# A hybrid block on one core: six more experts' weights in the tiles of x, whose rows pass through the first expert sum

## The reference

```python
probs = softmax(x @ router_w.T)                  # 64 experts
topk_w, topk_ids = top_k(probs, 8)               # 8 a token, at most 128 tokens an expert
xb = x_buf[:E * C].reshape(E, C, -1)             # gathered rows, 128 an expert
h = silu(einsum("ecd,edf->ecf", xb, w_gate)) * einsum("ecd,edf->ecf", xb, w_up)   # f = 192
y = einsum("ecf,efd->ecd", h, w_down)
routed = segment_sum(y[safe] * weight, tok)      # each row back to its token
shared = silu(sg) * su @ ws_down                 # a dense part for all tokens
x = x + routed + shared
```

## Time and profile before

| what | value |
|---|---|
| median of 3 runs | 2984.09 us (2981.26 to 2991.69) |
| profiled execution | 2984.79 us, span 2983.0 us |
| busy PE, DVE, ACT, POOL | 82%, 78%, 58%, 34% of the span |
| mean granted TensorE clock | 0.916 |
| DMA | 293.69 MB, mean 98 GB/s |
| shared part of f1 / expert loop of f1 | about 1602 to 1690 / 1690 to 1938 us |

### The profile page before, as it was taken

The page is one execution under the profiler, slowest core; times in us unless marked ns, Lnnn a source line. Parts: engine busy times, 40 slices in busy tenths (PEclk is TensorE's granted clock), DMA queues, the critical chain, the costliest instruction groups (busy, mean ns, idle before and its releaser), DMA issues. The chain is left out here.

```text
span 2983.0 us, 45953 instructions
## 1 busy us (share of the span) xinstructions
PE 2443.0 (82%) x14814; PEld 1084.2 (36%) x14814; DVE 2322.8 (78%) x3787; ACT 1715.9 (58%) x3510; POOL 1000.6 (34%) x755
## 2 busy tenths in 40 slices
PE   8899999999999999999767877737476676597772
PEld 5322222222222222222155566612122222456662
DVE  7898999999999999999158633338799998693333
ACT  3257888888888888888624322226465564532221
POOL 4500000000000000000202566652798996146662
PEclk9789999999999999999977998957899899598996
DMA  4423111111111111111434198770443441226997
GB/s 154 127 84 106 48 48 48 45 35 40 47 48 48 46 36 38 47 48 27 154 104 145 50 240 224 169 112 13 101 114 101 113 113 54 98 61 175 238 236 203
DMA packets 255164, 293.69 MB, mean 98 GB/s; under 512 B 39120, under 2 KB 210448, under 8 KB 254928
## 3 DMA queue, kind: packets, MB, share of 16 engines
q1 hardware_dynamic: 213664, 235.09, 27.4%
q0 software_dynamic: 33104, 46.42, 8.6%
q10 hardware_dynamic: 8160, 9.32, 1.0%
HBM read 223.35 MB, written 66.75 MB: 97 GB/s over the span
## 5 line engine op out<-in xcount | busy, mean ns | idle before, releaser
L745 DVE TENSOR_REDUCE att_mx<-att_pR 128x1 f32<-128x512 f32 x2048 | 1266.5, 684 | 33.5 <-PE att_pR L785 33.1
L728 ACT ACTIVATE att_probs<-att_pS 128x512 f32<-128x512 f32 x2048 | 1064.0, 603 | 231.2 <-PE att_pS L815 231.0
L832 PE MATMUL att_pA<-att_probs,att_vh 128*17 128x512 f32 x4096 | 539.5, 598 | 12.6 <-ACT att_acc_sb L709 12.2
L815 PE MATMUL att_pS<-att_q,att_k 64*128 64x512 bf16 x1344 | 458.0, 379 | 1.0 <-ACT att_probs L728 0.7
L2173 PE MATMUL sc_pY<-sc_hc,all_ident 128*128 128x512 f32 x512 | 263.4, 639 | 125.9 <-DVE sc_hc L2130 98.9
L2039 POOL TENSOR_TENSOR sc_bh<-ssm_du,sc_b 128x1024 f32<-128x1024 f32 x128 | 297.8, 2361 | 10.2 <-issue 5.6
L672 POOL TENSOR_TENSOR att_neg<-att_mx,att_minus 128x16 f32<-128x16 f32 x32 | 7.1, 223 | 842.4 <-DVE att_mx L753 842.4
L785 PE MATMUL att_pR<-head_k,head_q 64*128 64x512 bf16 x704 | 257.5, 403 | 13.7 <-PEq L71 7.1
L815 PE MATMUL att_pS<-head_q,head_k 64*128 64x512 bf16 (+1 forms) x1408 | 263.3, 381 | 0.2
L815 PE MATMUL att_pS<-att_qs,att_ks 64*128 64x512 bf16 x1344 | 261.1, 377 | 0.3
L785 PE MATMUL att_pR<-att_ks,att_qs 64*128 64x512 bf16 x672 | 259.3, 386 | 0.0
(11 more groups left out here) (303 smaller groups left out, 3884.5 us busy)
## 6 DMA issues: line engine op xcount, KB each, us to landing
sc_b<-scan_rows SPq DMA_DIRECT2D x128, 256.0 KB, 3.3
expert_sum<-att_zeros SPq DMA_DIRECT2D x4, 4224.0 KB, 21.2
f1e_wgu<-in_w_gate SPq DMA_DIRECT2D x64, 192.0 KB
f1e_wgu<-in_w_up SPq DMA_DIRECT2D x64, 192.0 KB
f2e_wgu<-in_w_gate SPq DMA_DIRECT2D x64, 192.0 KB
f2e_wgu<-in_w_up SPq DMA_DIRECT2D x64, 192.0 KB
sc_c<-scan_rows SPq DMA_DIRECT2D x40, 256.0 KB, 3.4
head_q<-query_parts SPq DMA_DIRECT2D x132, 64.0 KB, 2.2
```

Source lines behind the costliest of these rows:

```text
L728: act.activation(probs[:, k % (2 * HALF), :], bank(place(k)), ACT.Exp, scale=float(DK) ** -0.5).then_inc(expd, 1)
L745: dve.tensor_reduce(mx4[s][:, k // QC, k % QC:k % QC + 1], pR[:, (s + k) % 3, :], AX.X, ALU.max).then_inc(maxed, 1)
L815: mm = pe.matmul(bank(place(k)), kk[rows, t * P:(t + 1) * P], q[rows, c * GROUP:(c + 1) * GROUP], start=not half, stop=bool(half))
L832: mm = pe.matmul(pA[32 * c:32 * c + DK + 1, :], vh[s][:, t, :], probs[:, (HALF * g + j) % (2 * HALF), :], start=(t == 0), stop=(t == KT - ...
```

## The change

In `phase_experts`, once a pair of tiles of `x_sb` has got its shared part, ACT stores it to the first sum in HBM (`to_memory`; in place of the zeros there). Its tiles then hold the weights of six more experts, five tiles each (`more_at`: expert 10 + k goes to half k % 2, tile 5 (k // 2)), so that the ring has 16 slots. Before each of these six loads SP waits until the stores that cover its tiles, and all before them in that half, have landed. POOL waits for all stores before its first indirect addition, and clears the padding of the six slots. The test `if n == WR` in front of `both` is not touched. Since x now sits in the first sum, the state-space phase reads it with plain SP loads (two ahead of its weights, six behind) and POOL adds only the second sum; the final merge loads the first sum straight into `x_sb` and adds once per group.

```diff
-    WR = 10
+    OWN, MORE = 10, 6
+    WR = OWN + MORE
...
+        SLOT_TILES = 5
+        def more_at(k):
+            return k % 2, (k // 2) * SLOT_TILES
+        def more_flat(k):
+            h, t = more_at(k)
+            return x_sb[:, HT * h + t:HT * h + t + SLOT_TILES, :].rearrange("p t d -> p (t d)")
...
                     sp.wait_ge(listed, 1)
                     sp.dma_start(both[:, CAP:2 * CAP], firsts[EXPERTS:P, :]).then_inc(moved, 16)
+                if OWN <= n < WR:
+                    h, t = more_at(n - OWN)
+                    for k in range((t + SLOT_TILES + 1) // 2):
+                        sp.wait_ge(in_memory[h][k], 16)
                 if n >= WR:
                     sp.wait_ge(down, n - WR + 1)
...
             for n in range(LEAD):
                 gather(n)
+            for h in range(2):
+                for n in range(N):
+                    pool.wait_ge(in_memory[h][n], 16)
+            for k in range(MORE):
+                pool.memset(wd[OWN + k][H:P, 1, :], 0.0).then_inc(more_padded, 1)
...
+            def to_memory(n, h):
+                act.wait_ge(s_added, n * 2 + h + 1)
+                rows = slice(HT * h + n * 2, HT * h + n * 2 + 2)
+                act.dma_start(dst[:, rows, :], x_sb[:, rows, :]).then_inc(in_memory[h][n], 16)
+
             def shared_y(n, h):
+                if n >= 1:
+                    to_memory(n - 1, h)
                 act.wait_ge(s_down, v(n * 2 + (h + 1)))
-                if not early(n, 1):
-                    act.wait_ge(s_added, v(n * 2 + (h - 1)))
...
-            turns(act, shared, N, 2, 2, N - 2)
+            for n in range(N):
+                shared(n, n % 2, n // 2, N - 1 - n)
             for h in range(2):
                 shared_y(N - 1, h)
+            for h in range(2):
+                to_memory(N - 1, h)
...
                 for q in range(2):
                     dve.wait_ge(s_in[q][n], 16)
-                    if q:
-                        dve.wait_ge(added, 2 * n + 1)
-                    dve.tensor_tensor(row, row, part[:, n, q, :, :], ALU.add).then_inc(added, 1)
+                dve.tensor_tensor(row, row, part[:, n, :, :], ALU.add).then_inc(added, 1)
...
+            load(0)
+            load(1)
             sp.dma_start(wdt[:, :, :], io["W_dt"].rearrange("(c p) r -> p c r", p=P)).then_inc(w_in, 16)
...
+            for n in range(2, GROUPS):
+                load(n)
...
-            def merge(n, q):
-                if q:
-                    pool.wait_ge(merged[0][n], 16)
-                src = sums[q][0:TOK, :].rearrange("(t p) d -> p t d", p=P)
+            def merge(n):
+                pool.wait_ge(merged[0][n], 16)
+                src = sums[1][0:TOK, :].rearrange("(t p) d -> p t d", p=P)
...
             def first_merges():
-                for n in range(GROUPS):
-                    merge(n, 0)
                 for n in range(4):
-                    merge(n, 1)
+                    merge(n)
```

More of the change, by code:

```diff
@@ L1300, in phase_experts @@
         s_y = m.sb("s_y", [P, 2, 2 * D])
-        wgu = m.sb("wgu", [P, WR, DC, 2 * FF])
-        wd = m.sb("wd", [P, WR, 2, D])
+        own_wgu = m.sb("wgu", [P, OWN, DC, 2 * FF])
+        own_wd = m.sb("wd", [P, OWN, 2, D])
         xg = [m.sb(f"xg{s}", [P, ROW]) for s in range(R)]
@@ L1326, in phase_experts @@
         w_in = [m.sem(f"w_in{s}") for s in range(WR)]
+        in_memory = [[m.sem(f"in_memory{h}_{n}") for n in range(N)] for h in range(2)]
+        more_padded = m.sem("more_padded")
         consts = m.sem("consts")
@@ L1338, in phase_experts @@
         block = ctx.enter_context(nc.Block())
+        SLOT_TILES = 5
[4 more added lines that the diff above has]
+            return x_sb[:, HT * h + t:HT * h + t + SLOT_TILES, :].rearrange("p t d -> p (t d)")
+        wgu, wd = [], []
+        for k in range(OWN):
+            wgu.append(own_wgu[:, k, :, :])
+            wd.append(own_wd[:, k, :, :])
+        for k in range(MORE):
+            wgu.append(more_flat(k)[:, 0:DC * 2 * FF].rearrange("p (c n) -> p c n", c=DC))
+            wd.append(more_flat(k)[:, DC * 2 * FF:DC * 2 * FF + 2 * D].rearrange("p (c d) -> p c d", c=2))
         @block.sync
@@ L1355, in _ @@
                 for k, name in enumerate(("w_gate", "w_up")):
-                    sp.dma_start(wgu[:, w, :, k * FF:(k + 1) * FF], io[name][n].rearrange("(p c) f -> p c f", c=DC))                      .then_inc(w_in[w], 16)
-                sp.dma_start(wd[:, w, 0, :], io["w_down"][n, 0:P, :]).then_inc(w_in[w], 16)
-                sp.dma_start(wd[0:H, w, 1, :], io["w_down"][n, P:FF, :]).then_inc(w_in[w], 16)
+                    sp.dma_start(wgu[w][:, :, k * FF:(k + 1) * FF], io[name][n].rearrange("(p c) f -> p c f", c=DC))                      .then_inc(w_in[w], 16)
+                sp.dma_start(wd[w][:, 0, :], io["w_down"][n, 0:P, :]).then_inc(w_in[w], 16)
+                sp.dma_start(wd[w][0:H, 1, :], io["w_down"][n, P:FF, :]).then_inc(w_in[w], 16)
         @block.gpsimd
         def _(pool):
-            pool.memset(wd[H:P, :, 1, :], 0.0).then_inc(padded, 1)
+            pool.memset(own_wd[H:P, :, 1, :], 0.0).then_inc(padded, 1)
             pool.memset(hh[H:P, :, 1, :], 0.0).then_inc(padded, 1)
@@ L1416, in _ @@
         def _(act):
+            dst = sums[0][0:TOK, :].rearrange("(t p) d -> p t d", p=P)
+            def to_memory(n, h):
+                act.wait_ge(s_added, n * 2 + h + 1)
+                rows = slice(HT * h + n * 2, HT * h + n * 2 + 2)
+                act.dma_start(dst[:, rows, :], x_sb[:, rows, :]).then_inc(in_memory[h][n], 16)
             def shared_y(n, h):
+                if n >= 1:
+                    to_memory(n - 1, h)
                 act.wait_ge(s_down, v(n * 2 + (h + 1)))
-                if not early(n, 1):
-                    act.wait_ge(s_added, v(n * 2 + (h - 1)))
                 act.activation(s_y[:, h, :], pY[:, h, :], ACT.Copy).then_inc(s_y_ready, 1)
@@ L1555, in down_product @@
                 for c in range(2):
-                    mm = pe.matmul(pY[:, n % 2, 0:D], hh[:, n % 2, c, :], wd[:, n % WR, c, :],
+                    mm = pe.matmul(pY[:, n % 2, 0:D], hh[:, n % 2, c, :], wd[n % WR][:, c, :],
                                    start=(c == 0), stop=(c == 1))
@@ L1567, in _ @@
                 pe.wait_ge(w_in[w], 64 * (n // WR + 1))
+                if OWN <= n < WR:
+                    pe.wait_ge(more_padded, n - OWN + 1)
                 if n >= 2:
@@ L1571, in _ @@
                     for c in range(DC):
-                        mm = pe.matmul(pG[:, q, k * CAP:(k + 1) * CAP], wgu[:, w, c, k * P:(k + 1) * P], xT[:, q, c * P:(c + 1) * P],
+                        mm = pe.matmul(pG[:, q, k * CAP:(k + 1) * CAP], wgu[w][:, c, k * P:(k + 1) * P], xT[:, q, c * P:(c + 1) * P],
                                        start=(c == 0), stop=(c == DC - 1))
@@ L1585, in phase_merge @@
         m = Mem(nc, ctx, tag)
-        part = m.sb("part", [P, GROUPS, 2, GT, D])
+        part = m.sb("part", [P, GROUPS, GT, D])
         s_in = [[m.sem(f"s_in{q}_{n}") for n in range(GROUPS)] for q in range(2)]
@@ L1596, in load @@
             src = sums[q][0:TOK, :].rearrange("(t p) d -> p t d", p=P)
-            eng.dma_start(part[:, n, q, :, :], group_of(src, n)).then_inc(s_in[q][n], 16)
+            eng.dma_start(part[:, n, :, :] if q else group_of(x_sb, n), group_of(src, n)).then_inc(s_in[q][n], 16)
         @block.sync
@@ L1604, in _ @@
             for n in range(GROUPS):
-                sp.wait_ge(added, 2 * n + 2)
+                sp.wait_ge(added, n + 1)
                 sp.dma_start(group_of(dst, n), group_of(x_sb, n)).then_inc(stored, 16)
@@ L1619, in _ @@
                     dve.wait_ge(s_in[q][n], 16)
-                    if q:
-                        dve.wait_ge(added, 2 * n + 1)
-                    dve.tensor_tensor(row, row, part[:, n, q, :, :], ALU.add).then_inc(added, 1)
-            dve.wait_ge(added, 2 * GROUPS)
+                dve.tensor_tensor(row, row, part[:, n, :, :], ALU.add).then_inc(added, 1)
+            dve.wait_ge(added, GROUPS)
 def ffn(nc, io, tag, x_sb, ident, table, sums, out):
@@ L1712, in _, with load @@
         def _(sp):
+            def load(n):
+                src = sums[0][0:TOK, :].rearrange("(t p) d -> p t d", p=P)
+                sp.dma_start(x_sb[:, n * GT:(n + 1) * GT, :], src[:, n * GT:(n + 1) * GT, :])\
+                  .then_inc(merged[0][n], 16)
+            load(0)
+            load(1)
             sp.dma_start(wdt[:, :, :], io["W_dt"].rearrange("(c p) r -> p c r", p=P)).then_inc(w_in, 16)
@@ L1733, in _ @@
         def _(pool):
-            def merge(n, q):
-                if q:
-                    pool.wait_ge(merged[0][n], 16)
-                src = sums[q][0:TOK, :].rearrange("(t p) d -> p t d", p=P)
+            def merge(n):
+                pool.wait_ge(merged[0][n], 16)
+                src = sums[1][0:TOK, :].rearrange("(t p) d -> p t d", p=P)
```

(8 more changed lines are left out.)

## The result

The changed kernel takes 3023.03 us (median of four runs, 3015.68 to 3023.65) beside 2985.64 for the kernel before (four runs): a ratio of 1.0118, 95% interval 1.0094 to 1.0142. The forecast was 3029.4, a rise of 44.6 us where 37.4 was measured. The profiled execution has a span of 3021.0, 38.0 over that of before.

What follows compares the result with a forecast made beforehand. Expert loops were taken as DMA-bound beside a shared part with idle DMA. 25.3 + 24.6 + 1.4 - 7.5 + 0.5 + 1.5 - 1.2 = +44.6 on 2984.8 gives 3029.4 us; eight times in ten 3013 to 3041.

Steps and rivals of the forecast that it cites:

- The held list chain: Hand-over to experts: `both` follows expert 15's weights, behind the last stores; first gather later by 25.3 (f1) and 24.6 us (f2).
- the time at which `both` leaves: Hand-over: SP issues `both` 6.4 us after the last shared addition, about 1696.1 in f1, with a store taken at 2.5.
- the queue ahead of `both`: Hand-over: `both` queues behind the weights of experts 14 and 15; 0.7 us a stage, +1.4, bounds 0 and 2.5 a stage.
- The worst case of 5 us a stage: Hand-over: all 1.15 MB of weights still ahead of `both` in its ring, the sum some 9 us higher.
- The loop: Expert loops: 48 experts' weights left to load, not 54; six experts move to 3.19 us each, together -7.5.
- POOL's 3.19: Tail of the expert loop: once the last weights are in, POOL's own two issues pace it at 3.19 us.
- The rival in which bytes count in full: Expert loops: bound by the bytes of the whole loop, 15.2 us saved a stage, total 3006; chance 8%.
- Covered work: Both stages: stores, unrolled ACT loop and POOL memsets are hidden and cost nothing; uncovered stores would be 8 us a stage.
- the longer pause of PE: Before the experts: PE idles some 30 us and not 5; costs nothing more, 2 us a stage at the most.
- the 0.5 us of more semaphores to clear: Both stages: twenty-three more semaphores to clear in each, +0.5 us in all, bounds 0 and 3.
- The entry of the state space: After f1: POOL's fourth merge waits for SP's fourth load, and DVE for POOL's root; +1.5 us, bounds -1 and +6.
- The final merge: After f2: one addition of 1.23 us behind the last load and not two; -1.2, bounds -2 and 0.

Runs made afterwards that it cites:

- Experiment 1: Changed kernel with one condition altered, so that `both` is issued after expert 9's weights (n == OWN) as in the kernel before: 2979.46 us, ratio 0.9987.
- 2: Kernel before with only an added SP wait for the last shared addition ahead of `both`: 3015.56 us, ratio 1.0110.
- experiment 3: Changed kernel with four extra slots (MORE = 4), so that `both` follows expert 13: 2993.59 us, ratio 1.0042.
- 4: Changed kernel with `both` issued after the waits of expert 14 but ahead of the weights of experts 14 and 15: 3012.53 us, ratio 1.0105.
- experiment 6: Experiment 1 without the transfer of w_gate for experts 16 to 63, computing with wrong gate weights: 2956.15 us, one run.
- Experiment 5: Changed kernel with no extra slot (MORE = 0), rows still passing through the first sum and `both` following expert 9: 2983.6 us, ratio 0.9996.
- experiment 9: Experiment 1 with SP's loads of groups 0 to 3 ahead of the small weights and POOL's memset of `sel` ahead of its first merge: 2969.7 us, ratio 0.9949.

## Why the forecast held, point by point

**The held list chain: right, shown.** The forecast rested on reading that an untouched `if n == WR` moves with WR. It named the order on SP's queue, the stores as what is waited for, and 26.0 and 25.3 us. It was 24.3 and 24.4. Experiment 1 takes it away, 2 makes it alone, 3 scales it, 4 splits it. The two uncertain terms, the time at which `both` leaves and the queue ahead of it, were both sized a little high. A store of 256 KB landed in 2.1 us and not 2.5:

```profile
expert_sum<-all_x ACTq DMA_DIRECT2D x32, 256.0 KB, 2.1
```

and `both` left 5.6 us after the last addition (1689.36 + 1.26 = 1690.62), not 6.4. The queue ahead of `both`, set at 0.7 a stage, was 0.2 to 0.3: it landed in 2.0 and 2.1 us, beside 1.8 in the kernel before. The worst case of 5 us a stage did not come, though experiment 3, with 2.7 and 3.6 us, shows that the term need not be small. The order within a ring that the Trainium skill describes (DMA: Bandwidth & Descriptors, Queues, rings and completion order) was of little matter in the changed kernel. A third part of the difference no term foresaw: from the first `slots` round to `ids` DVE took 16.0 us in f1 and not 16.8 (f2 16.0 and 16.1); the cause was not looked for.

**The loop: mechanism right, total a little more than forecast.** Forecast -7.5, measured -10.0 in this pair of traces and -10.2 over all loops. The main interval stayed: from expert 9 to 47 it is 3.84 and 3.81 us, where the kernel before has 3.83 and 3.79 on the same stretch, and experts wait for gathered rows as before. The forecast put its 4.0 and 3.5 us a stage behind expert 47, where six experts no longer have weights loaded beside them. From there to the last `y` all loops with ten slots took 53.1 us on average, with 14 slots 51.1, with 16 slots 49.6: 3.4 a stage less, about as forecast. In this pair alone it is 7.0 and 2.9, as the two loops of one kernel differ there by up to 4 us. What the sum lacked is another 1.6 a stage between experts 9 and 47 (means 144.7 and 143.1), and that is too near the spread of single loops (139.4 to 147.1) to call; its cause is open. One reading in the forecast was rough: POOL's 3.19 does not hold to the end, since the last two experts go in 2.2 and 1.2 us. They do so in both kernels, so it drops out of the difference. The rival in which bytes count in full, 15.2 a stage, is out; experiment 6 points to a reason, weight bytes that take less DMA time than the average of the loop. My own reading, that the loop is DMA time at one price per byte, was too simple too, but the sum did not use it.

**Covered work: right.** Stores, unrolled loop, memsets and the longer pause of PE were put at nothing. Experiment 5, which has the stores and the unrolled loop, shows no cost that can be measured (ratio 0.9996); it has neither the memsets nor the pause. For these stands the changed kernel itself: its first experts took 11.5 and 11.4 us to the first `y`, as before, with PE's clock at 0.50 for the first 4 us either way:

```profile
1718.00:1722.00 4.00, 3.31 (x15) 2.98 (x16) 0.00 (x0) 0.77 (x2) 3.50 (x9) 0.50 0.42 122
```

For the 0.5 us of more semaphores to clear the forecast had no row; the stretches from the last `y` to the next phase grew by 0.2.

**The entry of the state space: direction right, +0.5 for +1.5.** POOL's last early merge was issued at 17.2 us after the start, 1.3 later than before, and the root followed POOL and not DVE, as the forecast said.

**The final merge: wrong by its 1.2.** One addition less behind the last load changed nothing: from its start to the end of the span the phase takes 38.4 us in both. The step that failed is that a shorter addition in the chain of waits shortens the end. The last addition did end earlier, 28.5 us after the start of the phase and not 28.9, but SP was not waiting for it. SP's own stream was behind: in both kernels it issues the eight stores of the result one behind the other. The last addition has ended at 2973.50 (before) and 3011.08 (after); SP is busy with the seventh store until 2973.91 and 3011.87, and the eighth follows at once, 29.4 and 29.3 us after the start of the phase. The kernel before, then the kernel after:

```profile
L1606 SPq DMA_DIRECT2D out_x<-all_x x8: 1165/2108/2926, 2958.3 to 2974.0; - x8
```
```profile
L1649 SPq DMA_DIRECT2D out_x<-all_x x8: 1163/2097/2916, 2996.3 to 3011.9; - x8
```

What makes such issues last 1.2 to 2.9 us each, I did not test.

**What stays open.** The stretch from the first root to f2 varied from 617.3 to 622.2 among kernels that do not differ in it (1.9 shorter in the changed kernel than before), which blurs sums to some 4 us; I have no cause for it. So is what holds the loop above POOL's pace with DMA at 0.85.

## What to carry to other kernels

When a ring grows, search for every condition that uses its length: work that was slotted in "after the ring is full" moves too, and on an in-order queue it takes along all waits in front of it. Before adding a wait to a queue, ask what small, urgent transfer stands behind it; here one of 32 KB on SP cost 49 us at the two hand-overs, and one changed condition took them back. And deeper prefetch into a loop that never waits for its weights mainly shortens the part of the loop that has weight traffic; price it as the difference of the two intervals, not as bytes over bandwidth. Last, a chain of waits that ends at an addition does not make that addition the end: look at what the queue behind it is doing when it is done.

## What the hardware showed that I had not expected

Long POOL operations on SBUF can hold a DVE operation until they end: 1.71 us became 5.91 beside a memset of 4.06, and 0.17 became 2.61 beside a select of about 4. POOL time that looks free is free only where DVE is idle or does work that is not held up: `MAX8` of the routing list took 2.30 us beside a memset of 2.23 and 2.29 without one, in the kernel before, and in experiment 9 four `BATCH_NORM_STATS2` took their usual 1.4 us beside a select. Moving the pieces of `sel` beside DVE cost 12 us; placing them where DVE had next to nothing to do brought some 10.
